# A macaron block with polynomial attention: first quads' q and k stored apart, the state product last, all jobs placed anew

## The chip, the cores and the metric

The kernel runs on one core of a Trainium2 chip. The metric is the device time of one launch in microseconds. It was run three times: 1919.88, 1920.25 and 1925.5 us, median 1920.25. The engines are PE (TensorE), DVE (VectorE), ACT (ScalarE), POOL (GpSimd) and SP, which issues the DMAs here.

## The reference

```
x: 4 x 2048 x 256, 16 heads of 16 columns, all float32
ffn(z)  = z @ W.T + b + (z @ V_r) @ C.T          (W 256 x 256, V_r and C of rank 32)
x = x + 0.5 * ffn(layernorm(x))                   (ln1, ffn)
q, k, v = split(layernorm(x) @ W_attn)            (ln2, qkv)
att = q @ k.T / 4, causal (-inf above the diagonal)
att = (x > 0 ? x^2 + 1 : -100 <= x <= 0 ? 1 - x/100 : 0) / 1000
x = x + (att @ v) @ W_proj                        (proj)
x = x + 0.5 * ffn(layernorm(x))                   (ln3, out)
```

## The kernel before, in words

**The arithmetic.** There is no softmax, so the linear part of the polynomial, for keys in earlier blocks of 128 columns, is a product with a running sum: the *state*, one matrix of k's rows times v per block of 128 positions. What is left for each score is a raise (max(s, 0) plus a constant) and a square. On the diagonal blocks the linear part is made score by score (`lin`) and masked.

**Chunks and quads.** The 8192 positions are 16 *chunks* of 512, four to a batch. A *quad* is the attention of four heads of one batch; there are 16. A quad has four *windows* (query chunks c = 0 to 3) with 4, 8, 12 and 16 *tiles*, a tile being 512 queries (fewer on the diagonal) by 128 keys by four heads. A tile is two *halves* of two heads each: 40 tiles, 80 halves a quad. A half has two score products, each in float pieces packed to 96 rows of bfloat16 (`qs`, `ks`), into one of two PSUM buffers; the raise is DVE's, or ACT's for the odd half of a shared tile; the square is POOL's and ACT's for a shared tile, ACT's alone for the others; three tiles later (LAG) `values` adds the tile's product with v to `y_ps`. ACT copies a window's y out at its end (`copy_y`) and SP stores it.

**Jobs.** Everything else is made of jobs. Per chunk: A is ln1, z1T (transposes), ffn, ln2, z2T; B is qT, k, v, kT, state, with the split of q and k in three bfloat16 pieces (`split`; on DVE for chunks 0 to 4, on POOL and ACT later); C is proj, ln3, z3T, out. A job uses one of two PSUM banks, is cut into pieces, one a slot, and is emptied by ACT or DVE some slots later.

**The order** is written out by hand. `order()` lays down 2132 *slots*. Each engine runs through the same slots and does its own part of each; all engines keep their own order, and semaphores alone tie them. Tables (`A_FULL` and so on) give the slot of every job within a stretch. First come 36 slots for A of chunk 0; then 40, 40, 40, 44 and 48 slots, each with B of chunk c and A of chunk c + 1, and in the last four of these also the halves of window c of the first quad, packed behind the first 14 to 20 slots of the stretch (`spread`). Then each quad has 80 slots, one half in each, with B and A of the chunks to come, and from quad 4 on C of a chunk that is done (`B_FULL`, `A_FULL`, `C_FULL`). The last chunks' C stand behind the last quad.

**Layernorm steps**, each at its slot of the table: four statistics on DVE; `aggregate` (bn_aggr, then L876 adds epsilon into `var`); ACT's root of `var` (L860); `scales` on DVE (reciprocal, `shift` in L885, the latter from two tensors in SBUF); four normalisations on POOL (L697); POOL's addition of half the bias.

**q, k and v on their way to a quad.** They go through DRAM: `parts` (all pieces of q and k of a chunk, 1536 KB) in one store when kT's split is done (L608), qT and v in one each, the state in one. For quad 0 `"kq"` then waits for all four stores and loads q, qT, state, k and v of the chunk. ACT may overwrite `qkT` and `parts` for the next chunk only when the store has landed (`parts_stored`, the wait ahead of L807). For the later quads the loads of window c are issued when the quad before has made its last score of it (`"q"`) or last used a key (`"k"`).

**The state product.** `values` starts a window's `y_ps` with the product of qT and the state: 4 blocks of 128 queries by 4 strips of 32 columns, `start` in the first.

**Setup.** All weights share the counter `w_loaded`, all constants `const_ready`; its last increment is bias_half (L684), which waits for all weights, and PE, DVE and ACT wait for it. ACT copies `w_ffn` out of PSUM (L782) before it starts its slots.

## Time and profile before

| | |
|---|---|
| median of the runs | 1920.25 us |
| the profiled execution | 1931.65 us |
| its span | 1929.9 us |
| PE busy | 1665.2 us, 86% |
| DVE | 1361.7 us, 71% |
| ACT | 1363.2 us, 71% |
| POOL | 1326.5 us, 69% |
| mean granted clock of TensorE | 0.965 of full speed |
| score products | 742.7 us busy |
| products with v | 597.8 us busy |
| SP's DMAs | 178.82 MB, 31.6% of 16 engines' span |

Busy time is an average over stages that have different limits. A stretch is read by how far the busiest engine is from its length and by what ends the waits in it.

### The profile page before, as it was taken

The page shows a single profiled execution, that of the slowest core. Times are in us where ns is not written, and L with a number is a line of the kernel's source. Part 1 is how long each engine was busy: PE and PEld are TensorE (multiplying, and loading weights), DVE is VectorE, ACT ScalarE, POOL GpSimd, SP SyncE. Part 2 cuts the span into 40 slices and gives each one's busy share as a digit, 9 for nine tenths or more (in the row PEclk, how much of TensorE's full clock was granted, in tenths as well). Part 3 has the DMA queues.
Part 4 walks back from the last instruction along what each step waited for, and adds up shares of the span by engine and source line. Part 5 has one row for each costly group of instructions (what it writes and reads, how often), then busy time and mean ns, then how long its engine had stood idle before and what let it go on. Part 6 is the DMA issues. An engine that isn't in the chain of part 4 may idle for free.

```text
span 1929.9 us, 66983 instructions
## 1 busy us (share of the span) xinstructions
PE 1665.2 (86%) x27158; PEld 814.6 (42%) x27158; DVE 1361.7 (71%) x3313; ACT 1363.2 (71%) x2178; POOL 1326.5 (69%) x1419
## 2 busy tenths in 40 slices
PE   4677789898989989898998989898898999898785
PEld 2343334343444435353443535344444444443342
DVE  1465677777777867778786777878676778787672
ACT  1244568787888777777877877777787788888561
POOL 3344558787778868777676877867677767686552
PEclk8888889999999999999999999999999999999897
DMA  2344433241424233341523334241324222323111
GB/s 75 124 128 129 114 106 108 83 110 49 133 67 136 85 103 95 99 132 50 159 66 111 87 106 128 71 135 57 117 86 130 86 72 80 82 73 78 49 37 59
DMA packets 155191, 183.14 MB, mean 95 GB/s; under 512 B 22012, under 2 KB 129660, under 8 KB 152836
## 3 DMA queue, kind: packets, MB, share of 16 engines
q1 hardware_dynamic: 154884, 178.82, 31.6%
q8 instruction: 221, 3.62, 0.8%
q14 instruction: 86, 0.70, 0.1%
HBM read 102.43 MB, written 76.30 MB: 93 GB/s over the span
## 4 chain that ended last, share of the span: by engine, by line
PE 54%; DVE 15%; ACT 12%; issue 8%; POOL 8%; DMA 2%; SPq 0%; ACTq 0%; POOLq 0%; DVEq 0%
PE y_ps L991 20%; PE score L991 16%; PE bank L991 14%; DVE rp L926 9%; ACT rp L831 4%; ACT rp L851 3%; PE bank L1017 3%; POOL rp L735 2%; POOL z L697 2%; ACT rp L847 2%; DVE lin L932 2%; DMA part_scratch<-parts 1%; POOL rp L710 1%; POOL parts L465 1%; DMA x1c<-x_scratch 1%
## 5 line engine op out<-in xcount | busy, mean ns | idle before, releaser
L926 DVE TENSOR_SCALAR rp<-score 128x512 f32<-128x512 f32 (+2 forms) x1728 | 944.1, 573 | 276.0 <-PE score L991 271.3
L991 PE MATMUL score<-qs,ks 96*32 96x512 bf16 (+3 forms) x10240 | 742.7, 354 | 137.8 <-DVE rp L926 74.6
L735 POOL TENSOR_TENSOR rp<-rp 128x1024 f32<-128x1024 f32 (+1 forms) x416 | 756.3, 1830 | 125.1 <-DVE rp L926 114.1
L831 ACT ACTIVATE rp<-score 128x512 f32<-128x512 f32 (+1 forms) x832 | 458.4, 592 | 267.8 <-PE score L991 266.2
L991 PE MATMUL y_ps<-rp,vt 128*16 128x512 f32 (+3 forms) x5120 | 597.8, 537 | 24.3 <-ACT rp L851 13.3
L991 PEld LDWEIGHTS score<-qs,ks 96*32 96x32 bf16 x10240 | 294.4, 96 | 547.9 <-DVE rp L926 266.8
L847 ACT ACTIVATE rp<-rp,rise 128x1024 f32<-128x1024 f32 (+1 forms) x416 | 462.6, 1144 | 1.7 <-POOL rp L710 1.7
L710 POOL TENSOR_SCALAR_AFFINE_SELECT rp<-rp 128x256 f32<-128x256 f32 (+1 forms) x384 | 185.2, 484 | 317.2 <-DVE rp L926 161.5
L851 ACT ACTIVATE rp<-rp 128x1024 f32<-128x1024 f32 (+2 forms) x224 | 291.1, 1305 | 131.4 <-DVE rp L926 66.0
L932 DVE SCALAR_TENSOR_TENSOR lin<-score,slope_mask 128x128 f32<-128x128 f32 x768 | 214.4, 279 | 0.0
L991 PEld LDWEIGHTS y_ps<-rp,vt 128*16 128x16 f32 x5120 | 134.4, 97 | 111.5 <-ACT rp L851 25.7
L991 PE MATMUL bank<-w_ffn,zT 128*32 128x256 f32 x2048 | 160.3, 401 | 5.4 <-ACT zT L791 5.4
L991 PE MATMUL bank<-w_qkv,z2T 128*32 128x256 f32 x2048 | 152.5, 388 | 11.2 <-ACT parts L808 11.2
L1017 PE MATMUL bank<-ident,z 128*128 128x128 f32 x384 | 72.7, 327 | 45.2 <-POOL z L697 42.9
L991 PE MATMUL y_ps<-lin,vt 128*16 128x128 f32 x2048 | 106.2, 276 | 0.0
L991 PEld LDWEIGHTS bank<-w_ffn,zT 128*32 128x32 f32 x2048 | 69.0, 115 | 79.6 <-issue 51.6
L697 POOL TENSOR_SCALAR z<-x,rstd_ln,shift_ln 128x256 f32<-128x256 f32 x128 | 72.6, 575 | 40.8 <-DVE shift_ln L885 39.3
L991 PEld LDWEIGHTS y_ps<-lin,vt 128*16 128x16 f32 x2048 | 61.5, 97 | 80.0 <-issue 67.8
L991 PEld LDWEIGHTS bank<-w_qkv,z2T 128*32 128x32 f32 x2048 | 67.3, 112 | 62.4 <-issue 28.0
L991 PE MATMUL bank<-w_out,y_c 128*32 128x256 f32 x1024 | 83.4, 400 | 11.8 <-DMA x1c<-x_scratch 11.8
L1017 PEld LDWEIGHTS bank<-ident,z 128*128 128x128 f32 x384 | 49.6, 164 | 88.5 <-issue 78.2
L697 POOL TENSOR_SCALAR z<-x_sb,rstd_ln,shift_ln 128x256 f32<-128x256 f32 x64 | 35.0, 558 | 68.2 <-DVE shift_ln L885 68.2
(78 smaller groups left out, 1360.0 us busy)
## 6 DMA issues: line engine op xcount, KB each, us to landing
part_scratch<-parts SPq DMA_DIRECT2D x16, 1536.0 KB, 7.5
qs<-part_scratch SPq DMA_DIRECT2D x384, 64.0 KB
ks<-part_scratch SPq DMA_DIRECT2D x384, 64.0 KB, 2.4
state_scratch<-st_new SPq DMA_DIRECT2D x16, 528.0 KB
st<-state_scratch SPq DMA_DIRECT2D x64, 132.0 KB
x_sb<-in_L_attn_x_dram SPq DMA_DIRECT2D x16, 512.0 KB, 4.4
x_scratch<-x SPq DMA_DIRECT2D x16, 512.0 KB, 5.4
qT_scratch<-qkT SPq DMA_DIRECT2D x16, 512.0 KB, 3.8
```

The source lines that it names most:

```text
L465: ins = eng.tensor_tensor(parts[:, i, 2, :], rest[:], parts[:, i, 1, :], ALU.subtract)
L697: ins = pool.tensor_scalar(dst[:, i, :], src[:, i, :], rstd[k][:, i:i + 1], shift[k][:, i:i + 1], ALU.mult, ALU.add)
L710: pool.affine_select(out=block, in_=block, compare_op=ALU.is_ge, fill=fill, base=0, pattern=[[0, heads_in_it], [1, P]], channel_multiplier ...
L735: pool.tensor_tensor(half, half, half, ALU.mult).then_inc(squared["pool"], 1)
L831: nc.scalar.activation(rp[T % RP_BUFS][:, 2 + v, off:CH], score[H % S_BUFS][:, v, off:CH], ACT.Relu).then_inc(raised["act"], 1)
L847: nc.scalar.activation(part, part, ACT.Square, bias=rise[:]).then_inc(squared["act"], 1)
L851: nc.scalar.activation(whole, whole, ACT.Square).then_inc(squared["act"], 1)
L926: nc.vector.tensor_scalar(rp[T % RP_BUFS][:, 2 * u + v, off:CH], score[H % S_BUFS][:, v, off:CH], 0.0, RISE, ALU.max, ALU.add).then_inc(ra ...
L932: nc.vector.scalar_tensor_tensor(lin[D % L_BUFS][:, 2 * u + v, :], score[H % S_BUFS][:, v, off:off + P], ONE / SLOPE, slope_mask[:, 0, :], ...
L991: return nc.tensor.matmul(*args, start=start, stop=stop, skip_group_check=True)
L1017: ins = nc.tensor.transpose(dst[:, P * blk:P * blk + P], src[:, blk, P * i:P * i + P], ident[:])
```

## The change

q and k of chunks 0 to 3 are also needed by quad 0. Now each gets its own store of what quad 0 needs (the first 128 columns, all pieces), a wait for it, and its loads; the rest of `parts` follows in a third store. qT, v and the state have counters and loads of their own (`load_qT`, `load_v`, `load_st`); for quad 0, qT and v are copied from SBUF to SBUF. For the later quads qT and the state are loaded when the window's last values are done. `values` makes the state product behind a window's last tile, in strips of 16 columns; the first tile's products start the bank, and `y_ps` is cleared once. All tables are new; the prologue's stretches are 36, 40, 42, 39, 44 and 48 slots, and the halves of quad 0 are spread from slot 69 to 249. `var` is gone: ACT takes the variance out of `mv` with epsilon as bias, and `aggregate` takes over the wait that guards `mv`. In the setup each weight group and each group of constants has a counter, DVE makes the fills, and ACT copies `w_ffn` just before it empties the first z1T.

```diff
-A_FULL = {"z1T": (32, 34), "ffn": (38, 42), "z2T": (61, 63), "ln1": 8, "ln2": 45}
-B_FULL = {"qT": (0, 6), "k": (8, 12), "v": (16, 20), "kT": (46, 52), "state": (48, 54, 56, 58)}
-C_FULL = {"proj": (24, 28), "ln3": 32, "z3T": (65, 67), "out": (71, 75)}
-A_FIRST = {"z1T": (12, 13), "ffn": (14, 18), "z2T": (34, 35), "ln1": 0, "ln2": 22}
-A_EARLY = {"z1T": (12, 13), "ffn": (14, 18), "z2T": (38, 39), "ln1": 0, "ln2": 22}
-B_EARLY = {"qT": (0, 2), "k": (4, 8), "v": (22, 26), "kT": (30, 32), "state": (31, 33, 34, 35)}
+A_FULL = {"z1T": (32, 33), "ffn": (36, 40), "z2T": (61, 63), "ln1": 10, "ln2": 45}
+B_FULL = {"qT": (0, 7), "k": (8, 12), "v": (16, 20), "kT": (45, 57), "state": (49, 59, 61, 63)}
+C_FULL = {"proj": (22, 26), "ln3": 30, "z3T": (69, 69), "out": (72, 76)}
+A_FIRST = {"z1T": (12, 13), "ffn": (14, 18), "z2T": (30, 34), "ln1": 0, "ln2": 24}
+A_EARLY = {"z1T": (12, 13), "ffn": (16, 20), "z2T": (38, 39), "ln1": 0, "ln2": 24}
+B_EARLY = {"qT": (4, 6), "k": (7, 8), "kT": (14, 15), "v": (26, 28), "state": (34, 35, 36, 37)}
+HALVES_AFTER = (33, 31, 31, 33)
+LENGTHS = (36, 40, 42, 39, 44, 48)
...
-    for c, (length, first) in enumerate(((40, 20), (40, 14), (44, 14), (48, 14))):
-        at = o.stretch(length, spread(first, length, 2 * (LAST[c] + 1 - FIRST[c])))
-        o.stage(c + 1, at, B_EARLY)
-        o.stage(c + 2, at, A_EARLY)
+    starts = []
+    for c, length in enumerate(LENGTHS[1:]):
+        at = o.stretch(length)
+        o.stage(c, at, B_EARLY)
+        o.stage(c + 1, at, A_EARLY)
+        if c < CPB:
+            starts.append(at + HALVES_AFTER[c])
+    starts.append(o.n)
+    for c in range(CPB):
+        o.put_halves(spread(starts[c], starts[c + 1], 2 * (LAST[c] + 1 - FIRST[c])))
...
+                    if what == "first q":
+                        c, = args
+                        cols = slice(CH * c, CH * c + CH)
+                        if c == 0:
+                            sp.wait_ge(filled, FILLED)
+                        wait_emptied(sp, "qT", c, 0)
+                        sp.dma_start(qT[1:QD + 1, cols], qkT[0:QD, 0, :]).then_inc(qT_loaded[c], 16)
+                        sp.wait_ge(split_step, 12 * c + 3)
+                        sp.dma_start(part_d[c, :, 0, 0], parts[:, 0, :, :]).then_inc(first_q_stored, 16)
+                        sp.wait_ge(first_q_stored, (c + 1) * 16)
+                        load_q(0, c, q_loaded[c])
+                    if what == "first k":
+                        c, = args
+                        sp.wait_ge(split_step, 12 * c + 9)
+                        sp.dma_start(part_d[c, :, 1, 0], parts[:, KC, :, :]).then_inc(first_k_stored, 16)
+                        sp.wait_ge(first_k_stored, (c + 1) * 16)
+                        load_k(0, c, k_loaded[c])
...
-            act.wait_ge(const_ready, CONSTS)
+            def empty_weights():
+                for k in range(KC):
+                    act.wait_ge(setup_pe, 2 + k)
+                    nc.scalar.activation(w_ffn[:, k, :], y_ps[k][:, 0:DM], ACT.Copy, scale=0.5).then_inc(setup_act, 1)
+                act.wait_ge(const_ready, CONSTS)
+                act.wait_ge(filled, FILLED)
...
-                        act.wait_ge(var_done[k], chunk + 1)
-                        nc.scalar.activation(sd[k][:], var[k][:], ACT.Sqrt).then_inc(sd_done[k], 1)
+                        act.wait_ge(aggr_done[k], (chunk + 1) * NB)
+                        nc.scalar.activation(sd[k][:], mv[k][:, :, 1], ACT.Sqrt, bias=eps[:]).then_inc(sd_done[k], 1)
...
-            dve.wait_ge(const_ready, CONSTS)
+            nc.vector.memset(eps[:], EPS)
+            for k in range(KC):
+                nc.vector.memset(y_ps[k][:], 0.0).then_inc(y_cleared, 1)
+            nc.vector.memset(st_new[:], 0.0).then_inc(filled, 1)
+            nc.vector.memset(k_sb[:], 1.0).then_inc(filled, 1)
+            nc.vector.memset(qT[:], 1.0).then_inc(filled, 1)
+            nc.vector.memset(y_sb[0][:], 0.0).then_inc(filled, 1)
...
-                dve.wait_ge(aggr_done[k], (chunk + 1) * NB)
-                nc.vector.tensor_scalar(var[k][:], mv[k][:, :, 1], EPS, None, ALU.add).then_inc(var_done[k], 1)
...
-                    for m in range(NB):
-                        strips(y[:, P * m:P * m + P], st[:, NB * c + m, :], qT[:, CH * c + P * m:CH * c + P * m + P],
-                               start=m == 0, stop=False)
...
+                if t == LAST[c]:
+                    pe.wait_ge(qT_loaded[c], (n + 1) * 16)
+                    pe.wait_ge(st_loaded[c], (n + 1) * 16)
+                    for m in range(NB):
+                        for head in range(QH):
+                            ins = mm(y[STRIP * head:STRIP * head + HD, P * m:P * m + P],
+                                     st[:, NB * c + m, STRIP * head:STRIP * head + HD],
+                                     qT[:, CH * c + P * m:CH * c + P * m + P], start=False, stop=m == NB - 1)
```

## Rows read from the trace of the kernel before

**Rows 1.** The page's slices of 48 us: granted TensorE clock in tenths.
```profile
PEclk8888889999999999999999999999999999999897
```

**Rows 2.** By stretch: length, each engine's busy us (instructions), clock, DMA share, GB/s.
```profile
0.00:42.37 42.37, 17.11 (x100) 10.79 (x101) 7.38 (x28) 6.77 (x12) 15.57 (x31) 0.93 0.29 86
42.37:74.06 31.69, 23.46 (x344) 12.87 (x345) 14.68 (x39) 9.16 (x18) 10.00 (x16) 0.88 0.22 67
74.06:115.57 41.51, 31.11 (x456) 17.41 (x457) 23.80 (x64) 14.44 (x29) 17.86 (x26) 0.84 0.41 132
115.57:166.78 51.21, 38.68 (x608) 21.20 (x609) 30.93 (x81) 23.59 (x41) 22.51 (x29) 0.86 0.39 122
166.78:227.81 61.03, 47.96 (x708) 22.46 (x711) 37.93 (x87) 29.88 (x51) 29.81 (x32) 0.87 0.41 136
227.81:293.69 65.88, 55.25 (x804) 25.01 (x793) 45.58 (x101) 39.55 (x62) 34.90 (x35) 0.87 0.41 114
293.69:396.27 102.58, 92.09 (x1560) 44.35 (x1561) 78.10 (x190) 83.39 (x135) 79.95 (x82) 1.00 0.32 95
...
714.81:826.82 112.01, 100.95 (x1698) 49.99 (x1698) 84.02 (x205) 85.19 (x137) 84.95 (x90) 0.98 0.35 101
...
1584.32:1674.93 90.61, 81.89 (x1352) 37.41 (x1353) 70.50 (x173) 76.58 (x116) 65.95 (x66) 1.00 0.28 75
```

**Rows 3.** The same view, stretches of quad 5.
```profile
714.81:772.47 57.66, 56.19 (x992) 29.73 (x996) 45.01 (x123) 44.92 (x80) 45.14 (x51) 1.00 0.37 108
772.47:802.35 29.88, 22.83 (x396) 10.47 (x388) 23.50 (x49) 20.31 (x32) 25.96 (x29) 0.98 0.24 63
802.35:809.02 6.67, 6.67 (x76) 3.07 (x76) 2.71 (x7) 5.91 (x12) 5.31 (x7) 0.85 0.83 290
```

**Rows 4.** Waits within 772.47 to 802.35: us in total, times, longest.
```profile
PEld score L991 <- DVE rp L926: 11.5, 14, 2.0
```

**Rows 5.** Timeline of the start: start us, us, engine, line, operation, idle.
```profile
1.21 1.81 POOL L659 MEMSET st_new<- 66x2048 f32 x1
...
3.86 0.52 POOL L661 MEMSET y_sb<- 128x512 f32 x1
...
12.24 1.41 DVE L951 BATCH_NORM_STATS2 bnst_ln<-x_sb 128x6 f32<-128x256 f32 x4 [12.24 <-POOL bias_half L684]
...
27.43 6.34 PE L991 MATMUL bank<-w_ffn,zT 128*32 128x256 f32 x64 [0.78 <-ACT zT L791]
```

**Rows 6.** The page's DMA issues: size, median us to landing.
```profile
part_scratch<-parts SPq DMA_DIRECT2D x16, 1536.0 KB, 7.5
...
ks<-part_scratch SPq DMA_DIRECT2D x384, 64.0 KB, 2.4
...
qT_scratch<-qkT SPq DMA_DIRECT2D x16, 512.0 KB, 3.8
```

**Rows 7.** Timeline: ACT's qT copy behind a parts store, first and last of three.
```profile
81.70 0.60 ACT L807 ACTIVATE qkT<-bank 128x512 f32<-128x512 f32 x1 [7.78 <-DMA part_scratch<-parts]
...
173.53 0.60 ACT L807 ACTIVATE qkT<-bank 128x512 f32<-128x512 f32 x1 [6.89 <-DMA part_scratch<-parts]
```

**Rows 8.** Timeline in quad 5: var, shift, POOL's squares, the state product, y's copy.
```profile
782.16 1.90 POOL L735 TENSOR_TENSOR rp<-rp 128x1024 f32<-128x1024 f32 x1 [0.58 <-DVE rp L926]
...
783.32 0.76 DVE L876 TENSOR_SCALAR var_ln<-mv_ln 128x4 f32<-128x4 f32 x1
...
785.82 3.75 POOL L735 TENSOR_TENSOR rp<-rp 128x1024 f32<-128x1024 f32 x2
...
786.66 2.93 DVE L885 SCALAR_TENSOR_TENSOR shift_ln<-mv_ln,rstd_ln 128x4 f32<-128x4 f32 x1
...
787.57 1.05 PE L991 MATMUL y_ps<-qT,st 66*32 66x128 f32 x32
...
789.21 0.60 ACT L817 ACTIVATE y_sb<-y_ps 128x512 f32<-128x512 f32 x1
```

**Rows 9.** Groups: the var step, count, busy us, mean ns, idle before.
```profile
L876 DVE TENSOR_SCALAR var_ln<-mv_ln 128x4 f32<-128x4 f32 x48 | 30.3, 631 | 1.6
```

More of the change, by code:

```diff
@@ L155, in stage, with put_halves @@
                 self.jobs.append(Job(kind, chunk, i, at + start))
+    def put_halves(self, slots):
+        for s in slots:
+            assert s not in self.halves
+            self.halves[s] = self.next_half
+            self.next_half += 1
     def stretch(self, length, slots=()):
-        for s in slots:
-            self.halves[self.n + s] = self.next_half
-            self.next_half += 1
+        self.put_halves([self.n + s for s in slots])
         at = self.n
@@ L348, in build @@
         mv = {k: sb(f"mv_{k}", [P, NB, 2]) for k in LNS}
-        var = {k: sb(f"var_{k}", [P, NB]) for k in LNS}
         sd = {k: sb(f"sd_{k}", [P, NB]) for k in LNS}
@@ L393, in build @@
         q_loaded = [sem(f"q_loaded{c}") for c in range(CPB)]
+        v_loaded = [sem(f"v_loaded{c}") for c in range(CPB)]
+        qT_loaded = [sem(f"qT_loaded{c}") for c in range(CPB)]
+        st_loaded = [sem(f"st_loaded{c}") for c in range(CPB)]
         qk_done = sem("qk_done")
@@ L569, in _ @@
                     put(x.empty_at + (2 if x.chunk < EARLY else 8), "parts", x.chunk)
-                    if x.chunk < CPB:
-                        put(x.empty_at + 5, "kq", 0, x.chunk)
+                if x.chunk < CPB:
+                    if (x.kind, x.i) == ("qT", 0):
+                        put(x.empty_at + 2, "first q", x.chunk)
+                    if (x.kind, x.i) == ("kT", 0):
+                        put(x.empty_at + 2, "first k", x.chunk)
+                    if (x.kind, x.i) == ("v", 1):
+                        put(x.empty_at + 1, "first v", x.chunk)
+                    if (x.kind, x.i) == ("state", NB - 1):
+                        put(x.empty_at + 7, "first st", x.chunk)
                 if (x.kind, x.i) == ("proj", 0):
@@ new lines, in slot @@
+                    if what == "first k":
[4 more added lines that the diff above has]
+                        load_k(0, c, k_loaded[c])
+                    if what == "first v":
+                        c, = args
+                        wait_emptied(sp, "v", c, 1)
+                        sp.dma_start(vt[:, NB * c:NB * c + NB, :], v_sb[:, 0, :, :]).then_inc(v_loaded[c], 16)
@@ L615, in slot @@
+                    if what == "first st":
+                        c, = args
+                        sp.wait_ge(st_zero, 16 * BATCH)
+                        sp.wait_ge(st_stored, (c + 1) * 16)
+                        load_st(0, c, st_loaded[c])
                     if what == "q":
@@ L779, in _ @@
             nc.scalar.activation(cT[:], score[0][0:32, 0, DM:2 * DM], ACT.Copy).then_inc(setup_act, 1)
-            for k in range(KC):
-                act.wait_ge(setup_pe, 2 + k)
-                nc.scalar.activation(w_ffn[:, k, :], y_ps[k][:, 0:DM], ACT.Copy, scale=0.5).then_inc(setup_act, 1)
-            act.wait_ge(const_ready, CONSTS)
+            def empty_weights():
[4 more added lines that the diff above has]
+                act.wait_ge(filled, FILLED)
             def empty(x):
@@ L957, in _ @@
             for s in range(o.again):
+                if s == o.place["z1T", 0, 0].empty_at:
+                    dve.wait_ge(const_ready, CONSTS)
                 slot(s)
@@ L1035, in job @@
                         pe.wait_ge(c_loaded, (a + 1) * 32)
+                    if first and kind == "ffn" and a == 0:
+                        pe.wait_ge(setup_act, 4)
+                    if first and kind == "proj" and a == 0:
+                        pe.wait_ge(out_loaded, 16)
                     if first and kind in ("ffn", "out"):
@@ L1042, in job @@
                 if kind == "qT":
+                    if first and a == 0:
+                        pe.wait_ge(qkv_loaded, 16)
                     if first:
@@ L1098, in values @@
                     ins = mm(y[STRIP * head:STRIP * head + HD, off:CH], vt[:, kb, HD * head:HD * head + HD],
-                             rp[T % RP_BUFS][:, head, off:CH], start=False, stop=t == LAST[c])
+                             rp[T % RP_BUFS][:, head, off:CH], start=t == FIRST[c], stop=False)
                 if t in DIAG:
```

128 lines of the change are left out of this document (76 added, 52 removed).

## The prediction

> **What bounds the kernel now.** I read the slices first: the granted clock stands at 0.8 in the first six of forty slices of 48 us and at 0.9 in nearly all the others [rows 1]; TensorE is not kept at work in the first 290 us. So the span was cut into its stages. The boundaries are the first qT job of chunks 0 to 4 (42.37, 74.06, 115.57, 166.78, 227.81 us) and the first of each quad's 640 score products [rows 2]. The reader is to see three things. Setup and chunk 0 take 42.37 us with PE busy for 17.11. The first quad is worked off between 74.06 and 293.69, 219.6 us, together with the qkv and ffn jobs of four more chunks. And a quad with its jobs takes 102.58 us (quads 1 to 3), 112.01 (4 to 10; seven stand like it) or 90.61 (13, with only proj, ln3 and out beside it) [rows 2].
>
> In a steady quad PE is busy for 100.95 of 112.01 us, DVE, ACT and POOL for 84 to 85 each. Cut in two, its first 57.66 us have PE at 56.19, the next 29.88 us at only 22.83 while POOL stands at 25.96 and DVE at 23.50 [rows 3]. The list of waits for these 30 us is led by score products held by the raise on DVE, 11.5 us [rows 4]. So TensorE bounds most of a quad, and a stretch of 30 us in it is bound by POOL and DVE, whose work piles up there: ln2, the st_new sums and the splits behind kT. The last quad and the drain behind it have C jobs whose tables the change leaves alone.
>
> **Setup.** Before, PE, DVE and the first statistics all wait for one counter that ends with bias_half at 12.2 us, behind the last weight; ffn starts at 27.43 [rows 5]. The change gives each its own counter, loads x first, and lets DVE do the fills. No DVE fill is in the trace; I take POOL's prices as the nearest rows: 1.81 for 66x2048, twice; 0.52 for 128x512, once, and once more for each of two PSUM banks; 128x1040 at twice 0.52. That is 6.2 us. From below they could cost a quarter of that (1.5), from above twice (12, and then nothing is gained on this branch). With 6.2 the statistics start at 7 instead of 12.2. PE starts when vr, c and w_in have landed, by their places in the queue at 6 to 8 instead of 12.2. The branches meet at ffn. The weight products and ln1 took 15.2 us from 12.2 to 27.43 partly in series, because ACT made the root only behind both w_ffn copies; the root is now ahead of them, so another 3 to 4 us go. ffn starts at 17.5 to 20: **-9 us** (-11 to -1).
>
> **Stretch of chunk 0** (31.69 us). kT moves to the front and x1 no longer waits for v. But the first score product now stands in PE's queue ahead of state and z2T of chunk 1, and it needs split, store, six loads. Nearest rows: the whole parts store lands in 7.5 us, a 512 KB store in 3.8, a ks load in 2.4 [rows 6]. A third of the store is taken at 3.8, six issues are 2.7 and the landing 2.4: 9 us after the split of kT, which comes near 59 in times of before, so 68; z2T then runs near 70 instead of 72.1. **-1 us** (-6 to +3).
>
> **Four stretches of the first quad** (41.5, 51.2, 61.0, 65.9, sum 219.6) [rows 2]. Two sides bound the gain. The smaller: three times ACT's copy of qT waits, from 7.78 down to 6.89 us, for the parts store of the chunk before [rows 7]. In the new order kT comes right behind k and its store is issued some 20 slots ahead of the next qT, so this wait goes. Of each wait some 3.5 us were needed anyway for the two qT jobs on PE, so 4 to 5 us each leave the chain: 13 us. The larger: a steady rate. One quad with its jobs is 102.58, three more sets of A and B jobs are each 112.01 - 90.61 = 21.4 us; 102.6 + 3 x 21.4 = 166.8 us against 219.6, so 53 us at most. What fills the gaps is that halves, formerly packed into the end of each stretch (8 in 20 slots, 32 in 34), are spread over nearly all slots from 69 to 249. Against the full gain: each stretch keeps its chain ln1, z, z1T, ffn, ln2, z, z2T, with 25 to 30 us in series, and DVE keeps all splits of chunks 0 to 4. I take 34, 43, 51 and 55 us, between the sides and nearer the steady one for the long stretches, which hold the most attention: 183. **-37 us** (-13 to -53).
>
> **Steady quads 1 to 10.** The state product changes its place: still 32 records, 1.05 us in all, per window [rows 8], with 16 columns of weights in place of 32. The same time on PE, and y's copy, at 789.21, started only behind the next window's state product (787.57 + 1.05), so the same product ahead of it is covered: 0. If that cover is gone, it is 0.9 us a window. The var step goes: 48 instructions of 631 ns on the mean, 30.3 us in all [rows 9], of which 27 fall in these ten quads. What they cost is mostly waiting: the one at 783.32 lasts 0.76 us and ends where POOL's square of 1.90 us from 782.16 ends; the shift behind it, 2.93 us, ends with POOL's next two squares [rows 8]. The following raise is late by it, in the very stretch where PE waits for DVE: about 0.5 of 0.6 us each, and only one or two of three per quad on the path, so 0.7 us a quad. The Trainium skill (SBUF — State Buffer, "Who interferes with whom") says that such a DVE instruction and a GpSimd one that reads SBUF lock each other out for the whole instruction; by this the shift, which stays, meets the lock that var met, and the sum would keep only the instruction itself. That is a rival below.
> The new table takes POOL's state sums and kT1 out of the bound 30 us (states 54, 56, 58 go to 59, 61, 63; kT1 52 to 57) and spreads ffn and proj over slots two earlier. POOL was busy 25.96 of 29.88 us there; three sums of 0.7 us and two splits of 1.2 leave, 4.5 us, of which DVE at 23.5 lets perhaps 2 to 3 be gained, and the stretch behind (6.67 us at a granted clock of 0.85) gets some of it back. I take 1.8. Together **-2.5 us a quad, -25 us** (-45 to +15: nine tenths of each quad are PE's own work, and tighter pairs such as z3T twice in slot 69 can leave PE waiting for ACT's copies).
>
> **SP.** The loads are the same in number; v, qT and st only count on their own, and each leaves behind its own wait. In steady quads nothing is needed sooner than half a quad later: 0. Quads 11 to 14 and the tail: fewer jobs, the var steps of ln3, and the last state product behind the last values: **-3 us** (-8 to +4).
>
> **Sum.** -9 - 1 - 37 - 25 - 3 = -75 us. The profiled execution took 1931.65 us (span 1929.9) and would take 1857; the median of the runs is 1920.25, so 1845 us.
>
> **Rivals.**
> 1. The new stalls in the quads take what the old ones gave. For: the quad's PE share of 0.9 leaves little, and every change of place moves waits. Against: the 30 us in which PE works 22.8. Setup and first quad alone: -47, 1873 us.
> 2. The lock passes from var to shift: the 0.7 us a quad that var's waits were counted at stay, and the shift, now earlier, meets a whole square more often, 0.5 us a quad more: -75 + 12 = -63, 1857 us. For: shift already takes 2.93 us behind a square. Against: it then waits for a later one anyway, whether var was there or not.
> 3. The first quad reaches the steady rate (-53, -6 for chunk 0's stretch) and the quads lose 4.5 us each: -9 - 59 - 45 - 5 = -118, 1802 us. Against: DVE alone was busy 138 us in the four stretches, and the chain of each chunk remains.
> 4. Only the waits named go, the halves fill nothing since DVE is late for them: -9 - 13 = -22, 1898 us.
> 5. The slower side: the SP queue becomes the chain. For each of chunks 0 to 3 SP now waits for q's store, issues, then waits for k's store, issues: 9 us each, 75 us in series, with x loads, v and state stores queued behind, and PE's queue held by the first score product. If all lies on the path and takes the cover too: -9 - 13 + 75 = +53, 1973 us; it decides from 22 us on the path upward. Against: SP issues for a third of a stretch, and 13 to 19 slots lie between kT0 and the first score.
>
> **Chances.** Forecast 0.48 (its own range 1828 to 1862), rival 1 0.20, rival 2 0.10, rival 3 0.12, rival 4 0.06, rival 5 0.04. Range 1812 to 1882: it holds the forecast, rivals 1 and 2, and about half of 3; 1898, the rest of 3 and the slower case are outside. A change under 0.3% (5.8 us) is not told from none. Faster 0.95, same 0.02 (the rim of 4 and 5), slower 0.03.
>
> **What would show it.** Right: ffn of chunk 0 starts before 20; no wait of ACT's qT for the parts store over 1 us; quad 1's first score at 235 to 260 instead of 293.7; quads 4 to 10 at 108 to 111 us; y's copy waits for nothing. Wrong: SP waits for its first stores lead the stretches, or first scores wait for ks (then rival 5 or part of it); quads at 112 or more (rival 1); shift longer than 0.95 us on the mean by 0.4 (rival 2). The forecast fails most likely in the steady quads, where each microsecond counts ten times.

## The result, and the profile after

The changed kernel takes 1782.09 us (median of 4 runs, 1779.15 to 1783.2); beside it the kernel before took 1922.88 (4 runs, 1919.88 to 1926.72). The ratio is 0.9264, with a 95% interval of 0.9241 to 0.9288: 7.4% faster, 141 us. The forecast was 75 us, its range ended at 1812: the direction and the first quad were right, the size was not. The profiled execution took 1781.97 us (span 1780.2), 149.7 us less in span than the one before. One of the five executions of a kernel further down (q and k stored whole) took 4086 us against 1800 to 1806 for the other four, so its stages are read from another execution of that kernel.

The page's slices, to be laid beside [rows 1], and the stages as in [rows 2] (length, busy us and instructions of PE, PEld, DVE, ACT and POOL, granted clock, DMA share, GB/s). The cuts are again the first qT job of each chunk and the first score product of a quad.

```profile
PEclk9999999999999999999999999999999999999997
```

```profile
0.00:33.30 33.30, 16.45 (x104) 10.57 (x107) 13.24 (x37) 7.14 (x13) 10.72 (x27) 0.95 0.36 109
33.30:63.60 30.30, 23.34 (x370) 12.38 (x373) 17.83 (x42) 10.41 (x21) 10.53 (x18) 0.94 0.47 152
63.60:101.00 37.40, 29.42 (x544) 17.53 (x548) 29.37 (x73) 18.41 (x36) 24.02 (x31) 1.00 0.53 162
101.00:145.30 44.30, 36.28 (x612) 18.83 (x605) 32.84 (x77) 25.13 (x44) 24.41 (x30) 0.96 0.51 157
145.30:198.00 52.70, 44.57 (x713) 22.97 (x717) 37.27 (x88) 31.82 (x53) 28.50 (x30) 0.94 0.37 117
198.00:247.26 49.26, 40.47 (x644) 19.48 (x637) 37.52 (x79) 30.78 (x49) 29.11 (x31) 0.97 0.34 111
247.26:342.80 95.54, 90.48 (x1560) 45.73 (x1561) 75.01 (x188) 83.66 (x135) 79.65 (x82) 1.00 0.37 105
634.59:735.56 100.97, 97.10 (x1700) 52.06 (x1696) 79.87 (x200) 85.15 (x138) 84.59 (x90) 1.00 0.39 112
1437.26:1525.70 88.44, 81.19 (x1352) 38.89 (x1356) 70.16 (x171) 75.82 (x116) 65.85 (x66) 1.00 0.30 77
```

Up to quad 1 the lines are what was forecast. Then comes the surprise: quad 5 (second line from the bottom) went from 112.01 to 100.97 us, and quad 1 from 102.58 to 95.54. Summed over the quads:

| part of the span, us | before | after | moved | forecast |
|---|---|---|---|---|
| setup, to qT of chunk 0 | 42.37 | 33.30 | -9.1 | -9 |
| chunk 0's stretch | 31.69 | 30.30 | -1.4 | -1 |
| the four stretches of quad 0 | 219.6 | 183.7 | -35.9 | -37 |
| quads 1 to 10 | 1090.1 | 996.0 | **-94.1** | **-25** |
| quads 11 to 14 | 381.8 | 371.5 | -10.3 | |
| quad 15 and the end | 164.3 | 165.4 | +1.1 | -3 with the line above |

Where in quad 5 do the 11 us come from? It was cut at its 80 slots (one score half each). Slots 46 to 62 went from 28.12 to 20.22 us and slots 72 to 80 from 12.40 to 9.85: 10.4 of the 11.0. The first fence is before, the second after, in the columns of [rows 3]:

```profile
775.32:803.44 28.12, 21.12 (x360) 10.06 (x352) 21.81 (x46) 18.89 (x30) 24.20 (x27) 0.96 0.26 68
814.42:826.82 12.40, 9.87 (x166) 4.46 (x158) 7.73 (x18) 9.33 (x10) 4.71 (x4) 1.00 0.16 44
```

```profile
694.34:714.56 20.22, 17.98 (x330) 9.36 (x330) 17.53 (x43) 17.73 (x29) 18.26 (x20) 1.00 0.31 92
725.71:735.56 9.85, 9.83 (x176) 5.52 (x169) 7.68 (x19) 8.66 (x12) 6.00 (x4) 1.00 0.68 223
```

The first stretch lies, but for its last microsecond, in the 30 us that the prediction read [rows 3]; the second it did not look at. No engine is near its limit in the second: of 12.40 us PE is busy for 9.87, ACT for 9.33, DVE for 7.73 and POOL for 4.71. So work that piles up does not bound this stretch, and the reader is sent to the order of work.

### The profile page after: what moved, and what is told of

Its sections match the earlier page's. It is cut to its first block, busy times and chain, and to the rows that moved or that the text cites. A ratio compares the mean times of both kernels' runs of the same rounds, so it can differ in the third digit from the quotient of the medians.

```text
span 1780.2 us, 67010 instructions
## 1 busy us (share of the span) xinstructions
PE 1610.6 (90%) x27158; PEld 834.3 (47%) x27158; DVE 1328.6 (75%) x3272; ACT 1364.4 (77%) x2178; POOL 1319.1 (74%) x1415
## 4 chain that ended last, share of the span: by engine, by line
PE 55%; DVE 16%; ACT 12%; issue 6%; POOL 6%; DMA 3%; SPq 1%; ACTq 0%; POOLq 0%; DVEq 0%
PE y_ps L1079 20%; PE bank L1079 16%; PE score L1079 16%; DVE rp L1012 9%; ACT rp L910 5%; ACT rp L926 3%; POOL rp L807 3%; PE bank L1105 3%; DVE lin L1018 2%; DMA x1c<-x_scratch 2%; POOL z L769 1%; DVE bnst_ln L1037 1%; ACT rp L930 1%; ACT lin L916 1%; POOL rp L782 1%
## 5 line engine op out<-in xcount | busy, mean ns | idle before, releaser
L1079 PE MATMUL score<-qs,ks 96*32 96x512 bf16 (+3 forms) x10240 | 725.1, 350 | 54.2 <-DVE lin L1018 22.7
L910 ACT ACTIVATE rp<-score 128x512 f32<-128x512 f32 (+1 forms) x832 | 463.5, 602 | 201.5 <-PE score L1079 199.5
L1079 PEld LDWEIGHTS score<-qs,ks 96*32 96x32 bf16 x10240 | 303.4, 96 | 432.7 <-DVE rp L1012 146.0
L1079 PEld LDWEIGHTS y_ps<-rp,vt 128*16 128x16 f32 x5120 | 143.2, 96 | 116.4 <-issue 38.3
L1105 PE MATMUL bank<-ident,z 128*128 128x128 f32 x384 | 64.2, 302 | 38.0 <-POOL z L769 34.9
L916 ACT ACTIVATE lin<-score 128x128 f32<-128x128 f32 x256 | 80.5, 314 | 0.0
L1105 PEld LDWEIGHTS bank<-ident,z 128*128 128x128 f32 x384 | 44.6, 151 | 70.4 <-issue 58.4
```

Source lines behind the costliest of these rows:

```text
L910: nc.scalar.activation(rp[T % RP_BUFS][:, 2 + v, off:CH], score[H % S_BUFS][:, v, off:CH], ACT.Relu).then_inc(raised["act"], 1)
L916: nc.scalar.activation(lin[D % L_BUFS][:, 2 + v, :], score[H % S_BUFS][:, v, off:off + P], ACT.Copy, scale=SLOPE, bias=ONE).then_inc(lin_d ...
L1079: return nc.tensor.matmul(*args, start=start, stop=stop, skip_group_check=True)
L1105: ins = nc.tensor.transpose(dst[:, P * blk:P * blk + P], src[:, blk, P * i:P * i + P], ident[:])
```

## The experiments

The ten quads 1 to 10 went down by 94.1 us where 25 were forecast. Three steps could hold the 69 us that were missed: the tables of the full quads, the var step, the state product's new place. Each was done alone on the kernel before, and the tables were undone in the changed one. Where an expectation speaks of T, it is the theory that the tables carry the gain; L is the one that the lock between DVE and POOL does; M that it takes both together.

**The var step alone on the kernel before.**

```diff
-                nc.vector.tensor_scalar(var[k][:], mv[k][:, :, 1], EPS, None, ALU.add).then_inc(var_done[k], 1)
+                        nc.scalar.activation(sd[k][:], mv[k][:, :, 1], ACT.Sqrt, bias=eps[:]).then_inc(sd_done[k], 1)
```

> The kernel before with one thing changed: the var step is gone, ACT's root takes the variance with epsilon as bias. Theory L (the lock): each var step ends with the POOL square beside it and delays the raises behind it, and it also sets when the shift runs into the next square. Then quads 4 to 10 fall from 112 to 107 us or less, quads 1 to 3 from 102.6 to 98 or less, and shift's sum falls from 45.7 us. Theory T (the placing): var costs what I priced it at, 0.7 us a quad: quads 4 to 10 stay at 111, 1 to 3 at 102, and the run at 1913. Theory M (only both together): less than 2 us a quad here, since shift still lasts 2.9 us where it stands.

Measured: 1912.37 us, 0.9921 of before [0.9902, 0.9941]; quads 1 to 10 take 13.4 us less. The shift's sum does not fall, as L had it: it is 49.1 us instead of 45.7, while var's own 30.3 [rows 9] are gone. T's figures are met, L falls: var is a small term (forecast 0.7 us a quad; 1.3 here).

**The three tables alone on the kernel before.**

```diff
-A_FULL = {"z1T": (32, 34), "ffn": (38, 42), "z2T": (61, 63), "ln1": 8, "ln2": 45}
-B_FULL = {"qT": (0, 6), "k": (8, 12), "v": (16, 20), "kT": (46, 52), "state": (48, 54, 56, 58)}
-C_FULL = {"proj": (24, 28), "ln3": 32, "z3T": (65, 67), "out": (71, 75)}
+A_FULL = {"z1T": (32, 33), "ffn": (36, 40), "z2T": (61, 63), "ln1": 10, "ln2": 45}
+B_FULL = {"qT": (0, 7), "k": (8, 12), "v": (16, 20), "kT": (45, 57), "state": (49, 59, 61, 63)}
+C_FULL = {"proj": (22, 26), "ln3": 30, "z3T": (69, 69), "out": (72, 76)}
```

> The kernel before with the three tables of the steady quads (A_FULL, B_FULL, C_FULL) of the changed kernel, var and the state product as they were. Theory T: the placing gives most of the 11 us a quad that the changed kernel shows (112.0 to 101.0; 102.6 to 95.4 in quads 1 to 3): quads 4 to 10 at 103 to 105, quads 1 to 3 at 96 to 98, run near 1850. Theory L: at most 4 us a quad, quads at 108 to 110, run at 1890. Theory M: under 4 us a quad.

Measured: 1822.2 us, 0.9465 [0.9444, 0.9486]. Quads 1 to 10 take 98.2 us less, the whole 94.1 and a little more, while quad 1 starts at 288.1 (293.7 before). That is more than T expected (quads 4 to 10 at 100.4 to 101.3 us against its 103 to 105), and neither L nor M is left as the main cause. The same two stretches of quad 5 in this kernel:

```profile
735.44:755.28 19.84, 17.71 (x330) 9.26 (x329) 17.92 (x44) 17.63 (x29) 18.27 (x20) 1.00 0.32 94
766.44:776.29 9.85, 9.83 (x177) 5.55 (x168) 7.67 (x19) 8.66 (x12) 6.00 (x4) 1.00 0.66 223
```

**The old tables in the changed kernel** (the same six lines, turned round).

> The changed kernel with the three old tables of the steady quads put back; setup, first quad, root and state product stay changed. Theory T: quads 4 to 10 go back to 108 us or more and quads 1 to 3 to 100 or more, run at 1840 to 1870. Theory L: quads 4 to 10 stay at 105 or less, run at 1820 or less. In both, quad 1's first score comes at 247 as in the changed kernel, since the first quad has tables of its own.

Measured: 1890.47 us, 0.9804 [0.9779, 0.983]. Quads 4 to 10 are back at 110.2 to 112.0 us; with the tables go 108 us, more than was expected from either side. So three lines of slot numbers hold about three quarters of the whole gain. What in them does it?

**The state product's place alone on the kernel before** (the product behind the window's last tile, with loads of its own for qT and the state).

```diff
-                    for m in range(NB):
-                        strips(y[:, P * m:P * m + P], st[:, NB * c + m, :], qT[:, CH * c + P * m:CH * c + P * m + P],
-                               start=m == 0, stop=False)
...
+                if t == LAST[c]:
+                    pe.wait_ge(qT_loaded[c], (n + 1) * 16)
+                    pe.wait_ge(st_loaded[c], (n + 1) * 16)
...
```

> The kernel before with the state product behind the last tile of a window (with its two loads of their own and the cleared PSUM banks), tables and var as they were. By the prediction this is worth nothing: quads within 0.5 us of before, run within 5 us of 1921. A third theory S: the 1.05 us of state product at a window's first tile held back the first values of the window and so the buffers of the raises; then 2 us or more a quad, run at 1900 or less.

Measured: 1946.18 us, 1.0102 [1.0084, 1.0121]: slower by 19 us. In the profiled execution, 9.8 us longer in span than before, quads 1 to 10 take 10.8 us more, and the start gains nothing to speak of (quad 1 at 292.6). Neither expectation was met, and the prediction's price of 0 was wrong; more of that below.

**Parity.** On PE an even slot runs a tile's values product (about 1 us) ahead of the slot's piece of a job. `empty_at` has DVE empty a job in the slot of its last piece, before that slot's raise. If that slot is even, DVE meets the emptying first, and it stands still until values and piece are through, with a finished score behind it. The kernel before shows it in the timeline of quad 5:

```profile
792.14 0.40 PE L991 MATMUL score<-qs,ks 96*32 96x512 bf16 x4 [0.40 <-DVE lin L932]
...
792.35 1.04 PE L991 MATMUL y_ps<-rp,vt 128*16 128x512 f32 x8
...
793.22 0.52 PE L991 MATMUL bank<-v_sb,k_sb 128*32 128x64 f32 x18
...
793.89 0.42 DVE L912 TENSOR_TENSOR st_add<-bank,smask 66x256 f32<-66x256 f32 x1 [1.31 <-PE bank L991]
794.24 2.47 DVE L926 TENSOR_SCALAR rp<-score 128x512 f32<-128x512 f32 x4
...
794.97 0.40 PE L991 MATMUL score<-qs,ks 96*32 96x512 bf16 x4 [0.69 <-DVE rp L926]
...
819.81 0.69 DVE L908 TENSOR_TENSOR x<-bank,x 128x512 f32<-128x512 f32 x1 [3.34 <-PE bank L991]
820.42 2.55 DVE L926 TENSOR_SCALAR rp<-score 128x512 f32<-128x512 f32 x4
```

The scores of 792.14 are done at 792.5 and DVE is free then; the raise for them starts at 794.24, behind st_add (state), and PE in turn waits for the raise. At 819.81 it is the emptying of an `out` job: 3.34 us idle, then four raises in a row. The old state slots 48, 54, 56, 58 are even, the new ones odd. An `out` job has four pieces, so its emptying falls in slot start + 3: 74 and 78 before, 75 and 79 after. Three kernels were to tell this (P in the expectations) from a mere pile-up of work on POOL and DVE (Q).

Odd slots alone, on the kernel before, each a slot from its old place:

```diff
-"state": (48, 54, 56, 58)
+"state": (49, 55, 57, 59)
-"out": (71, 75)
+"out": (72, 76)
```

> The kernel before with only two rows moved by a slot or less: state from (48, 54, 56, 58) to (49, 55, 57, 59), out from (71, 75) to (72, 76). The values of a tile stand in even slots, ahead of the job pieces of the slot. Theory P (parity): DVE empties a state job in the slot of its piece and an out job in that of its last piece, ahead of its raise; in an even slot it waits there for PE's values product, with a score ready. Then halves 46 to 62 of a quad fall from 28.1 us to 23 or less, halves 72 to 80 of quads 4 to 10 from 12.4 to 10.5 or less, and the run to 1870 or less. Theory Q (load): the sums and ln2 together are too much for POOL and DVE wherever they stand within these slots; then halves 46 to 62 stay above 26 us, 72 to 80 above 12, and the run above 1900.

Even slots in the changed kernel, each a slot earlier:

```diff
-"state": (49, 59, 61, 63)
+"state": (48, 58, 60, 62)
-"out": (72, 76)
+"out": (71, 75)
```

> The changed kernel with only the same two rows put on the other parity: state from (49, 59, 61, 63) to (48, 58, 60, 62), out from (72, 76) to (71, 75); the sums stay as late and as spread as in the change. Theory P: halves 46 to 66 of a quad get longer by 4 us or more (from 24.6), halves 72 to 80 go back from 9.8 to 12 or more, quads 4 to 10 at 107 or more, run at 1840 or more. Theory Q: less than 2 us a quad, run at 1800 or less.

And the rest of the tables with parity left alone, that is the new A_FULL line only:

```diff
-A_FULL = {"z1T": (32, 34), "ffn": (38, 42), "z2T": (61, 63), "ln1": 8, "ln2": 45}
+A_FULL = {"z1T": (32, 33), "ffn": (36, 40), "z2T": (61, 63), "ln1": 10, "ln2": 45}
```

> The kernel before with the row of A jobs alone (z1T 32, 33; ffn 36, 40; ln1 10). Theory P: it changes no parity of a job that DVE empties; halves 46 to 62 stay at 26 us or more, and the gain is what the changed tables show in halves 30 to 46, 1 to 2 us a quad, run at 1900 to 1912. Theory Q: ffn's last emptying no longer meets ln2's statistics on DVE, and halves 46 to 50 fall from 6.2 to the 4.1 us of the changed tables, with 2 us or more of the following; run at 1885 or less.

Measured: odd slots 1876.29 us, 0.9736 [0.9707, 0.9765], quads 4 to 10 at 106.0 to 106.2; even slots 1854.55, 0.9629 [0.9595, 0.9662], quads at 107.7 to 108.4; the A line 1906.07, 0.989 [0.9854, 0.9925], quads at 108.5 to 110.3. Odd slots gave slightly less than P's bounds (23.95 us against 23 in slots 46 to 62, 1876 against 1870). With even slots the run and the quads fell inside P's bounds, the two stretches just outside: slots 46 to 66 went up by 3.6 us, not 4, and slots 72 to 80 to 11.60, not 12. The A line fell inside. Q's bounds are missed in all three. The two stretches of quad 5, in this order:

```profile
762.71:786.66 23.95, 19.64 (x361) 9.68 (x354) 21.02 (x46) 18.74 (x30) 20.63 (x25) 1.00 0.31 79
797.89:808.38 10.49, 9.73 (x177) 4.70 (x172) 7.51 (x17) 8.54 (x10) 5.06 (x4) 1.00 0.33 86
```

```profile
713.98:736.43 22.45, 18.71 (x330) 8.75 (x329) 16.35 (x42) 18.11 (x29) 19.73 (x22) 1.00 0.32 83
750.18:761.78 11.60, 9.69 (x165) 5.08 (x158) 6.97 (x14) 7.56 (x9) 3.79 (x2) 1.00 0.25 74
```

```profile
765.39:791.82 26.43, 20.09 (x360) 9.51 (x352) 21.54 (x46) 19.18 (x30) 23.48 (x27) 1.00 0.26 71
802.39:814.79 12.40, 9.86 (x165) 4.48 (x158) 7.73 (x18) 9.32 (x10) 4.70 (x4) 1.00 0.17 45
```

One slot's shift is worth 4.2 + 1.9 us one way and 2.2 + 1.8 (more with the slots behind) the other; of these two stretches the A line touches only the first. In the new tables parity is worth as much as in the old ones: with even slots quads 1 to 10 take 1048.3 us, 52.3 more than in the changed kernel.

But a shift by one slot also changes the order on PE. So in the next kernel no job was moved, and only DVE's emptying of state and out jobs came one slot later, on the kernel before (state from chunk 5 on, out of chunks 0 to 11):

```diff
+        late = (self.kind == "state" and self.chunk > CPB) or (self.kind == "out" and self.chunk < NCH - 4)
-        return self.start + PIECES[self.kind] + (1 if self.who == "act" else -1)
+        return self.start + PIECES[self.kind] + (1 if self.who == "act" else 0 if late else -1)
```

In the expectation, O is the theory that the order on PE is what counts.

> The kernel before with every job where it was; only DVE's emptying of state jobs (chunks 5 on) and out jobs (chunks 0 to 11) stands one slot later, so behind the raise of the half that PE scores ahead of the job, and in an odd slot. Theory P: the cost of the old table was DVE waiting for a piece behind values with a score ready, not PE's order: halves 46 to 62 fall from 28.1 to 25 us or less, halves 72 to 80 from 12.4 to 11 or less, quads 4 to 10 to 108 or less. Theory O (the order on PE is what counts, the pieces in even slots lengthen PE's own chain): less than 1 us a quad.

Measured: 1874.88 us, 0.973 [0.9696, 0.9765]; quads 1 to 10 take 46.3 us less, as with odd slots (45.2). PE's jobs stand where they stood, so O falls. Its two stretches, and its timeline at the place quoted above:

```profile
761.69:785.64 23.95, 19.32 (x361) 9.50 (x354) 20.93 (x46) 18.53 (x30) 20.63 (x25) 1.00 0.32 79
797.31:806.92 9.61, 9.29 (x164) 4.43 (x160) 7.25 (x17) 7.74 (x10) 4.62 (x4) 1.00 0.29 84
```

```profile
777.31 1.04 PE L992 MATMUL y_ps<-rp,vt 128*16 128x512 f32 x8
...
777.79 1.27 DVE L927 TENSOR_SCALAR rp<-score 128x512 f32<-128x512 f32 x2
...
778.17 0.52 PE L992 MATMUL bank<-v_sb,k_sb 128*32 128x64 f32 x18
...
778.99 0.41 DVE L913 TENSOR_TENSOR st_add<-bank,smask 66x256 f32<-66x256 f32 x1
```

DVE works through the values product, and st_add starts without idle time. The waits of the whole span fit (us in total, times, longest): before, after, even slots, late emptying.

```profile
DVE x L908 <- PE bank L991: 67.1, 32, 8.8
...
DVE st_add L912 <- PE bank L991: 40.6, 40, 3.1
```

```profile
DVE x L994 <- PE bank L1079: 40.8, 32, 8.8
...
DVE st_add L998 <- PE bank L1079: 13.9, 35, 1.0
```

```profile
DVE st_add L998 <- PE bank L1079: 63.2, 47, 2.1
DVE x L994 <- PE bank L1079: 60.4, 32, 8.8
```

```profile
DVE x L909 <- PE bank L992: 25.6, 19, 8.8
...
DVE st_add L913 <- PE bank L992: 13.4, 8, 3.1
```

Not all of the waiting goes: with the late emptying st_add waits 30.5 us for POOL's sums, where it waited 15.9 before.

Parity changes one thing more. In an odd slot of a shared tile the raise is ACT's, so DVE has none of its own behind the emptying; that holds for the slots 49, 55, 59, 61, 63 and 75. The last two slots of a quad part the two: that tile is whole, and DVE raises in both. Slot 79 took 1.48 us before (mean of quads 4 to 10), 0.55 with odd slots and 0.14 with the late emptying, and slot 78 1.40 in all three. So there the time is gained with the same engine raising before and after; how the gain in the other slots divides between the two was not run.

So about half of the tables' gain is shown to come from where DVE's emptyings of state and out jobs stand in their slots. The other half (a quad of 106 against one of 101) holds the A line (2.1 us a quad when alone) and all the rest of the three lines, the wider spacing of state and kT, and the new places of qT, proj, ln3 and z3T. For the spacing there is a sign: with odd slots alone, st_add waits 24.1 us for POOL's sums (12 times), with the full tables 0.4. None of this rest was run alone, so its share is what is left over, not a measurement.

**var put back into the changed kernel.**

```diff
-                        nc.scalar.activation(sd[k][:], mv[k][:, :, 1], ACT.Sqrt, bias=eps[:]).then_inc(sd_done[k], 1)
+                nc.vector.tensor_scalar(var[k][:], mv[k][:, :, 1], EPS, None, ALU.add).then_inc(var_done[k], 1)
```

> The changed kernel with the var step put back between the aggregation and the root. If its worth in the steady quads depends on the placing (nothing in the new tables: quads were 100.4 to 101.3 there with var in the old kernel), quads 4 to 10 stay at 101 to 102 and the run within 6 us of 1782. If it has a worth of its own of 0.6 to 0.7 us a step on the path, as I priced it, the run is at 1790 or more.

Measured: 1790.31 us, 0.9291 [0.9259, 0.9322], quads 1 to 10 at 999.5 against 996.0. The medians differ by 8 us, but they come from different comparisons, and the interval of the ratio overlaps the changed kernel's: a small term, not told from zero. So the two cases of the expectation are not parted: quads 4 to 10 at 101.5 to 102.5 us fit the first, the run fits the second by a hair.

**The first quad.** Its total was as forecast; three kernels ask which part carries it. Quad 1's start moves by some microseconds by itself: three kernels that leave everything ahead of it alone (the changed kernel again, with the old tables, with even slots) have it at 247.8, 249.7 and 252.8 us, against 247.3. The state product back at the window's first tile:

```diff
-                if t == LAST[c]:
+                if t == FIRST[c]:
                     pe.wait_ge(qT_loaded[c], (n + 1) * 16)
                     pe.wait_ge(st_loaded[c], (n + 1) * 16)
```

> The changed kernel with the state product at the first tile of a window again (strips of 16 columns and own loads kept). State last alone cost 1.1 us a quad in the old kernel (1100.9 against 1090.1 for ten quads) and old setup with new tables had its ten quads in 991.9 against 996.0. If that is the product's place, the ten quads come to 993 or less and the run to 1778 or less, unless the first quad, where the state now has to be there before a window's first values, loses it again: then quad 1 starts at 250 or more instead of 247. By my prediction the place is worth nothing: 1779 to 1785.

Measured: 1801.36 us, 0.935 [0.9321, 0.9379]. Quad 1 starts at 277.6, 30 us later, while quads 1 to 10 take 8.3 us *less* (987.7). The waits of its first 290 us name a cause for 21 of the 30 us: PE stands for the state's way through memory.

```profile
PE y_ps L1079 <- DMA st<-state_scratch: 21.1, 3, 8.1
```

The halves of the first quad packed into the ends of the stretches, as before:

```diff
-        o.put_halves(spread(starts[c], starts[c + 1], 2 * (LAST[c] + 1 - FIRST[c])))
+        first = ends[c] - LENGTHS[c + 2] + (20 if c == 0 else 14)
+        o.put_halves(spread(first, ends[c], 2 * (LAST[c] + 1 - FIRST[c])))
```

> The changed kernel with the first quad's halves packed as before: window c behind the first 20 or 14 slots of the stretch after its chunk's (8 in 22, 16 in 25, 24 in 30, 32 in 34 slots), all jobs and stores as changed. I forecast 183 us from chunk 1's qT to quad 1 (it is 183.7) and put the gain down to the wait for the parts store (13 us) and to the filled gaps (24 us). If so, quad 1 starts 20 to 28 us later, at 267 to 275, and the run is at 1802 to 1810. If the early stores were the whole, it stays below 255 and 1790.

Measured: 1794.68 us, 0.9311 [0.9281, 0.9341], quad 1 at 257.5. A miss: quad 1 comes 10 us later, half of the least that was expected and only twice what the start moves by itself.

q and k stored whole again, behind the last kT, with one store and the loads behind it:

```diff
-                        sp.dma_start(part_d[c, :, 0, 0], parts[:, 0, :, :]).then_inc(first_q_stored, 16)
...
-                        sp.dma_start(part_d[c, :, 1, 0], parts[:, KC, :, :]).then_inc(first_k_stored, 16)
...
+                        sp.wait_ge(parts_stored, (c + 1) * 16)
+                        load_q(0, c, q_loaded[c])
+                        load_k(0, c, k_loaded[c])
```

> The changed kernel with q and k of chunks 0 to 3 stored in one piece again when kT is split (1536 KB), and q and k loaded behind it; tables and halves as changed. The store lands in 5.6 to 7.5 us instead of 4, starts one split later and holds SP once instead of twice. By my terms this costs up to 5 us at each chunk's first score, where 13 to 19 slots of cover stand in front: 0 to 3 us for chunks 1 to 3, 4 to 6 for chunk 0: quad 1 at 250 to 256, run at 1785 to 1792. If the separate stores carry the gain of the first quad: quad 1 at 260 or later.

Measured: 1804.43 us, 0.9365 [0.9336, 0.9394]. A miss the other way: 3 to 10 us were expected, and the kernel is some 20 us slower. Its stages are those of the same kernel run again.

> The same kernel as the one with q and k stored in one piece, for its stages: its run is 22 us above the changed kernel, where I expected 3 to 10. If q and k that land late hold the first quad, quad 1 starts near 268 and the first scores wait for ks or qs; if the stall is elsewhere (ACT's next qT behind the loads), the scores do not wait for DMAs.

Measured: 1803.37 us; quad 1 at 270.2. In 30 to 280 us its scores wait for the loads, which in the changed kernel cost 0.8 us once:

```profile
PE score L1074 <- DMA qs<-part_scratch: 10.3, 2, 7.8
PE score L1074 <- DMA ks<-part_scratch: 8.4, 1, 8.4
```

**The state product where each quad wants it.** Its place at the end of a window is worth 30 us in quad 0 and costs 0.8 us in each later quad. So: last in quad 0, first in quads 1 to 15.

```diff
+                if t == FIRST[c] and n > 0:
+                    add_state(True)
...
+                if t == LAST[c] and n == 0:
+                    ins = add_state(False)
```

> The changed kernel with the state product behind the last tile in quad 0 alone and at the first tile, as before, in quads 1 to 15. State first had the ten steady quads in 987.7 against 996.0 us, but started quad 1 at 277.6 against 247.3, since values waited for st three times, up to 8.1 us. Two places, two effects: if both stand by themselves, quad 1 starts at 247 to 249, the ten quads take 987 to 990, and the run is 7 to 9 us under the changed kernel beside it. If the gain in the quads came from a shift in phase that only follows a late first quad, it is within 3 us of the changed kernel.

> The changed kernel itself, as the measure for the one beside it: 1779 to 1784 us, quad 1 at 247, ten quads in 996.

Measured side by side: 1771.89 us, 0.9207 [0.9177, 0.9237], against 1782.04, 0.9259 [0.9231, 0.9287], for the changed kernel. Quad 1 starts at 246.8 and 247.8, quads 1 to 10 take 986.3 and 994.3. The intervals overlap slightly, but the slowest of the five executions (1778.96) is below the fastest of the other's six (1779.16), and 8 of the 10 us lie in the quads, where the mechanism puts them. It is the best version found.

## Why the prediction was right in one half and wrong in the other

**Setup: right.** -9.1 against -9. ffn of chunk 0 starts at 19.08 (forecast 17.5 to 20), the statistics at 8.05 (forecast 7):

```profile
2.59 1.76 DVE L954 MEMSET st_new<- 66x2048 f32 x1 [0.41 <-issue]
...
4.52 0.93 DVE L955 MEMSET k_sb<- 128x1040 f32 x1 [0.17 <-issue]
...
8.05 1.34 DVE L1037 BATCH_NORM_STATS2 bnst_ln<-x_sb 128x6 f32<-128x256 f32 x4
...
19.08 2.36 PE L1079 MATMUL bank<-w_ffn,zT 128*32 128x256 f32 x20 [0.78 <-ACT zT L866]
```

The fills cost 1.76, 1.76, 1.03, 0.93 and 0.48 us, 6.0 together against the 6.2 taken from POOL's rows; issue gaps between them and the start made up the last microsecond.

**First quad: right in size, not in its parts.** 183.7 us against 183, the stretches 37.4, 44.3, 52.7 and 49.3 against 34, 43, 51 and 55; quad 1 at 247 in the window of 235 to 260. The waits of [rows 7] are gone; what they were worth was not run alone. They were 7.78, 7.32 and 6.89 us, so with 3.5 us each kept they hold 11.5 us, not the 13 of the sum. The filling by spread halves, which was to carry most, is worth about 10 us; the apart stores 23 and the state product's place 30 (each removed alone, so they overlap). For the state product the prediction had 0: it looked for its cover in a steady quad only, where st is loaded half a quad ahead. In quad 0 the state comes fresh out of a store and a load, and with the product first three windows stood 21.1 us for it. That the sum came out right is therefore partly luck: a term of 0 and a term too large met.

No term of the prediction holds another part of it. The four stretches, before and after:

```profile
74.06:293.69 219.63, 173.00 (x2560) 86.09 (x2561) 138.24 (x330) 107.46 (x182) 105.07 (x122) 0.86 0.41 125
```

```profile
63.60:247.26 183.66, 150.74 (x2504) 78.81 (x2505) 137.00 (x314) 106.14 (x178) 106.03 (x120) 0.96 0.43 134
```

22 of the 36 us are PE's busy time, with nearly the same number of instructions and a granted clock of 0.96 instead of 0.86. By the clock alone 173.0 us would become 155 (an estimate, 173.0 x 0.86 / 0.96). Filling PE's gaps and the clock went together here, and no run parts them.

**Steady quads: wrong, by 69 us.** The step that failed is "POOL was busy 25.96 of 29.88 us there; three sums of 0.7 us and two splits of 1.2 leave, 4.5 us, of which DVE at 23.5 lets perhaps 2 to 3 be gained [...] I take 1.8." It took [rows 4], scores held by the raise, as a sign of too much work on POOL and DVE, and priced the work that leaves. The work was not the bound: moving only DVE's emptyings, with no work less, gave 4.6 us a quad. DVE, at 23.50 of 29.88, had the time, but stood still at emptyings that its order puts ahead of the raise, and PE stood for the raise behind them. On the mean of the ten quads the full tables alone gave 9.8 us: odd slots alone give 4.5 of them, the A line alone 2.1, and 3.2 are left to what was not run alone, the spacing and the other rows. The changed kernel keeps 9.4, with the state product's place against it (0.8) and the missing var step for it (0.4). The 2.55 us of slots 72 to 80 were in no row of the prediction at all. It read the longest soft spot and not the others.

Nor is all of the gain idle time of PE. Quads 1 to 10, before and after:

```profile
293.69:1383.79 1090.10, 981.42 (x16552) 480.61 (x16553) 821.22 (x1987) 848.20 (x1362) 833.63 (x876) 0.99 0.34 98
```

```profile
247.26:1243.26 996.00, 952.12 (x16553) 502.53 (x16557) 784.05 (x1959) 847.84 (x1362) 830.35 (x876) 1.00 0.38 108
```

PE's idle time went from 108.7 to 43.9 us, by 64.8, and its busy time by 29.3 for the same number of instructions. The granted clock, 0.99 and 1.00, explains only a part: with odd slots alone PE is busy for 969.0 us in these quads at 1.00, with the full tables alone for 950.1 at 1.00.

The two other terms of the quads: var, forecast at 0.7 us a quad, was worth 1.3 on the kernel before and 0.4 on the changed one; the state product, forecast at 0, costs 1.1 and 0.8. The bound of 0.9 us "if that cover is gone" was per window, 3.6 a quad, and the measured cost lies inside it; the value taken, 0, was too low.

**The rivals.** Rival 3 (1802 us) was the closest in total and wrong in both halves: the first quad did not reach the steady rate. Rival 1 is excluded by the full tables alone: -98 us in the quads. Rival 2, the lock that passes on to the shift, is half true: with var taken out alone the shift's sum rises from 45.7 to 49.1 us, by 3.4 of var's 30.3. How long the shift takes depends on its place: its sum is 24.1 us with the new tables alone, 28.7 in the changed kernel.

```profile
L971 DVE SCALAR_TENSOR_TENSOR shift_ln<-mv_ln,rstd_ln 128x4 f32<-128x4 f32 x48 | 28.7, 599 | 1.6
```

By the Trainium skill (SBUF — State Buffer, "Who interferes with whom") a DVE instruction with two inputs in SBUF contends with a GpSimd one that reads SBUF, and the access that they share is an exclusive lock. The trace agrees: the same shift takes 0.16 us in the setup and 2.93 beside POOL's squares [rows 8]. It doesn't follow that the lock costs the time of its instructions: the 27 us of var and shift that the run without var took off DVE shortened the kernel by 14. Rival 4 was right in that the filled gaps give little, and wrong in its total. Rival 5 did not come: in the first quad PE's scores waited 0.8 us in all for their loads. Rival 5's own sum has 75 us where eight waits of 9 us make 72; it changes nothing here.

**The range** missed 1782 because the steady quads got a lower side of -45 us. That equals ten times the 4.5 us of work that leaves the stretch; the same -45 stands in rival 3. A wider bound was in the rows: 112.01 - 100.95 = 11.1 us in which PE is idle in a quad. Even that would not have been a floor, since PE's busy time fell too.

## What to carry to other kernels

Where two engines run by a list of slots, look at the order inside a slot on both: an emptying that stands ahead of an engine's critical work waits for all that its producer does ahead of it, and one slot later it may cost nothing. When an engine waits for another that isn't full, price the idle time, not only the work that leaves; ask what the other waits for, and look at every soft stretch of the loop. A product placed late to hide a transfer is worth its place only where the transfer is late; elsewhere it lengthens the end of the window.

## What the runs showed of the chip that was not expected

- Where PE's gaps shrank, its busy time shrank with them. In slots 46 to 62 of quad 5 the same 360 records were busy for 21.12 us at a granted clock of 0.96 before, and for 20.09 us at 1.00 with the new A line alone; with odd slots (361 records) it was 19.64 and with the late emptying 19.32, also at 1.00. That is 1 to 1.8 us beside the idle time, in a stretch of 28, and not all of it is the clock.
- DVE fills 66x2048 f32 in 1.76 us, POOL in 1.81 [rows 5]; 128x512 in 0.48 against 0.52. The two differ by less than a tenth here.
- The emptyings of state and out jobs, moved on DVE by a single slot with the same instructions, moved the kernel by 2.7%.
